# Moving most of the attention output projection into the last attention unit

## The chip, the cores and the metric

The kernel runs on one core of a Trainium2 chip. The metric is the device time of one execution in microseconds (us), median of several runs. Profiled times come from one execution that the hardware profiler recorded.

## The reference

The input is x of shape (4, 1024, 128): 4096 rows of 128 features. The model is

```
x = x + 0.5 * FFN(layernorm(x))
x = x + Attention(layernorm(x))
x = x + 0.5 * FFN(layernorm(x))
```

Both feed-forward steps use the same weights. FFN has a gate (8 experts, the two best of each row by a sigmoid score), eight experts of width 64, `silu(x Wg) * (x Wu)` and a down product, masked by the choice and scaled by one mean weight per expert, plus a shared expert of width 128. Attention has 16 query heads and 4 key heads of size 8, a causal mask and a bias that is linear in the distance with a slope per head. Its 128 output features go through `out @ Wo + bo`. All values are float32. Layernorm has no weights, only mean, variance and `1/sqrt(v + 1e-5)`.

## The kernel before

**Tiling.** The 4096 rows are 32 tiles of 128, in 8 groups of 4 tiles (512 rows, `GROUPS`, `GT`). The 4 batches and 4 key heads give 16 attention units (`UNITS`); unit i belongs to batch i // 4. Batch b holds groups 2b and 2b + 1. Each engine has its own written-out instruction stream, and semaphores order them. An engine executes its stream strictly in order, so an instruction that waits holds back all behind it. PSUM has 8 banks of 128x512 float32.

**Stages.** First feed-forward up (`ffn_up(f1, ...)`) and down (`ffn_down(f1, True)`), the latter with the projections to queries, keys and values; attention (`attention`); output projection (`out_proj`); second feed-forward (`ffn_up(f2, ...)`, `ffn_down(f2, False)`).

**An attention unit** has 12 steps (`STEPS`): four key tiles for the first 512 queries and eight for the second 512. In step s TensorE (PE) computes, at lines 1270 to 1304, the scores of step s + 1 in two pairs of heads (`score`, banks 3 to 6); between them maxima work of the next unit (`piece`, ring of banks 0 to 2), which the last unit, 15, hasn't; then the products of the exponentials of step s - 2 with the values (`times_v`, bank 7, `LAG` = 2). ScalarE (ACT) computes one exponential per pair (line 653) and copies bank 7 out when half a unit is complete (`out_evac`, line 642: for the unit before in step 3, for the first half of this one in step 6). A pair of scores may only be written when the exponential of the same pair of the step before has read the bank. `out_T` (steps 4 and 6, line 1220) turns the copied outputs, and VectorE (DVE) divides them by the row sums into `attn` (`normalise`, line 977). In unit 15 VectorE has little else to do. After the last unit come `times_v` of its last two steps, its last `out_evac`, `out_T` and `normalise`.

**Output projection** (`out_proj`, DVE lines 1019 to 1045, PE lines 1310 to 1326, ACT lines 663 to 668). For each group c: `gather` (DVE) brings 512 rows of `attn` into `sg`, `attention_T` (PE, four 128x128 transposes) turns them, ACT copies them to `yT`, PE multiplies by `wo` (four products of 128 columns), and `residual` (DVE) adds them to x. All of it waits for the last `normalise` (`dve.wait_ge(a_on, 2 * UNITS)`). Groups alternate between two banks each for turned outputs and for products.

**Second feed-forward, up.** In `front` group c has `statistics` (DVE, `ln_stats`, line 718), `rsqrt` (POOL), `ln_apply` (DVE, line 730), four transposes (PE), a copy to `xnT_all` (ACT, line 585), the gate's `logits` (PE) and up to two tiles of products `up(k)` (PE: one for `wg` and one for `wu`, 512 columns each, `front_tiles(c)`: none for group 0, one for group 1, two for each later group), `silu` (ACT) and `hidden` (DVE, line 746). The remaining tiles follow the eight groups. Tiles come in the order `TILE_ORDER`, whose first tiles belong to group 0. `xn` has room for one group, so `ln_apply` of a group waits for the transposes of the one before. `keep_running(n)` (PE, line 1328) issues n products of 512 columns whose result nobody reads: five ahead of the second feed-forward, two behind its first transposes.

Of the kernel before, what the change touches and what calls it, by code (L numbers as in the profile page):

```python
# [12 lines left out]
P = 128  # L13
# [71 lines left out]
WARM_FIRST, WARM_SECOND = 3, 5  # L85
# [35 lines left out]
W0_STEP = 5  # L121

# [54 lines left out]
def macaron(nc, dram, out):  # L177
    ctx = ExitStack()
    with ctx:
# [153 lines left out]
        def bank(b):  # L333
            return ps[:, b, :]

# [220 lines left out]
        def _(act):  # L556
# [20 lines left out]
            def ffn_up(f, load_constants):  # L577
                def silu(k, b):
                    act.wait_ge(f.G, k + 1)
                    after(act, f.h, k - 1)  # L580
                    act.activation(sg[:, b, :], bank(3 + b), ACT.Silu).then_inc(f.sg, 1)  # L581

                def front(c, par, first, last):
                    act.wait_ge(f.T, c + 1)
                    act.activation(xnT_all[:, c, :], bank(7 * par), copy).then_inc(f.xA, 1)
                    for k in front_tiles(c):
                        silu(k, k % 2)
                    if load_constants and c == GROUPS - 2:
                        constants()

                over_groups(front)
                act.wait_ge(f.lg, GROUPS)
                act.activation(sc, lg, ACT.Sigmoid).then_inc(f.sig, 1)
                for k in range(FRONT_END, len(TILE_ORDER)):
                    if k == SEL_AT:
                        act.wait_ge(f.mT, 1)
                        act.activation(selT.rearrange("p a n -> p (a n)"), ps[:, 2, 0:P].bitcast(BF16), copy)\
                           .then_inc(f.mk, 1)
                    silu(k, k % 2)
# [63 lines left out]
            def out_proj():  # L663
                def body(c, par, first, last):
                    act.wait_ge(o_T, c + 1)
                    after(act, o_y, c - 1)
                    act.activation(yT[:, par, :], bank(par), copy).then_inc(o_aT, 1)
                over_groups(body)

            ffn_up(f1, True)  # L670
# [3 lines left out]
            out_proj()  # L674
            ffn_up(f2, False)
# [4 lines left out]
        def _(dve):  # L680
# [57 lines left out]
            def ffn_up(f, first_ffn):  # L738
                ch = Chain(dve, f.ch_up)
                LN_LINKS, TOP_LINKS = 2, 17  # L740
# [8 lines left out]
                def statistics(c, par):  # L749
                    ch.at(LN_LINKS * c)  # L750
                    if first_ffn:
                        dve.wait_ge(s_x[c], 16)
                    ln_stats(c, par, ch, f.ve)
# [91 lines left out]
                statistics(0, 0)  # L845
# [13 lines left out]
            def ffn_down(f, qkv):  # L859
                ch = Chain(dve, f.ch_down)  # L860
                LN_LINKS, SPLIT_LINKS = 2, 2
# [114 lines left out]
            def attention(last_split):  # L976
# [42 lines left out]
            def out_proj():  # L1019
                def gather(c, b, half, par):  # L1020

                    after(dve, o_T, c - 1)
                    src = attn[:, bass.ds(KVH * b, KVH), GT * half:GT * half + GT, :]
                    dve.tensor_copy(sg[:, par, :].rearrange("p (t g e) -> p g t e", t=GT, g=KVH), src)\
                       .then_inc(o_an, 1)

                def residual(c, par):
                    dve.wait_ge(o_y, c + 1)
                    dve.tensor_tensor(xt(c), xt(c), bank(2 + par).rearrange("p (t f) -> p t f", t=GT), V.add)\
                       .then_inc(o_x, 1)  # L1030

                dve.wait_ge(a_on, 2 * UNITS)
                dve.wait_ge(o_bo, BO_PARTS)
                gather(0, 0, 0, 0)
                gather(1, 0, 1, 1)
                gather(2, 1, 0, 0)
                residual(0, 0)
                gather(3, 1, 1, 1)
                residual(1, 1)
                for b in range(1, BATCH - 1):  # L1040
                    gather(2 * b + 2, b + 1, 0, 0)
                    residual(2 * b, 0)
                    gather(2 * b + 3, b + 1, 1, 1)
                    residual(2 * b + 1, 1)
                residual(GROUPS - 2, 0)
                residual(GROUPS - 1, 1)
                dve.wait_ge(o_x, GROUPS)

            ffn_up(f1, True)
            last_split = ffn_down(f1, True)  # L1050
            attention(last_split)
            out_proj()
            ffn_up(f2, False)
# [4 lines left out]
        def _(pe):  # L1058
# [9 lines left out]
            def ffn_up(f, between):  # L1068
                def up(k):
                    b = k % 2  # L1070
                    c, tile = TILE_ORDER[k]
                    xT = xnT_all[:, c, :]
                    after(pe, f.sg, k - 1)
                    mm(bank(3 + b), wg[:, tile, :], xT).then_inc(f.G, 1)
                    after(pe, f.h, k - 1)
                    mm(bank(5 + b), wu[:, tile, :], xT).then_inc(f.U, 1)

                def logits(c, par):
                    pe.wait_ge(f.xA, c + 1)
                    after(pe, f.lg, c - 1)  # L1080
                    for t in range(GT):
                        ins = mm(ps[:, 1 + par, EXPERTS * t:EXPERTS * t + EXPERTS], xnT_all[:, c, t * P:(t + 1) * P],
                                 gate_w[:, :])
                    ins.then_inc(f.gl, 1)

                def front(c, par, first, last):
                    pe.wait_ge(f.xn, c + 1)
                    after(pe, f.xA, c - 1)
                    turn(lambda t: xn[:, t, :], 7 * par).then_inc(f.T, 1)
                    if first:  # L1090
                        keep_running(between)
                    else:
                        logits(c - 1, 1 - par)
                    if c == 1:
                        pe.wait_ge(s_w, 16 * len(ffn_loads))
                    for k in front_tiles(c):
                        up(k)
# [16 lines left out]
                logits(GROUPS - 1, 1)  # L1114
                for k in range(FRONT_END, len(TILE_ORDER)):
# [4 lines left out]
                    up(k)  # L1120
# [137 lines left out]
            def attention():  # L1258
# [11 lines left out]
                def body(i, par, first, last):  # L1270
# [8 lines left out]
                    for s in range(NSTEP):  # L1279
# [20 lines left out]
                        if s == OT0_STEP:  # L1300
                            out_T(i, 0)
                        if s == W0_STEP and not last:
                            maxima_T(i + 1, 0)

                over_units(body)
# [4 lines left out]
            def out_proj():  # L1310
                def attention_T(c, par):
                    pe.wait_ge(o_an, c + 1)
                    after(pe, o_aT, c - 1)
                    turn(lambda t: sg[:, par, t * P:(t + 1) * P], par).then_inc(o_T, 1)

                def body(c, par, first, last):
                    if not last:
                        attention_T(c + 1, 1 - par)
                    pe.wait_ge(o_aT, c + 1)
                    after(pe, o_x, c - 1)  # L1320
                    for t in range(GT):
                        ins = mm(ps[:, 2 + par, t * P:(t + 1) * P], yT[:, par, t * P:(t + 1) * P], wo[:, :])
                    ins.then_inc(o_y, 1)

                attention_T(0, 0)
                over_groups(body)
# [9 lines left out]
            ffn_up(f1, 3)  # L1336
# [3 lines left out]
            out_proj()  # L1340
            keep_running(WARM_SECOND)
# [59 lines left out]
```

## Time and profile before

| | us |
|---|---|
| median of 3 runs | 728.12 (727.83 to 728.29) |
| profiled execution, its own time | 728.65 |
| its span, from first to last instruction | 726.8 |
| TensorE busy | 699.3 (96%) |
| VectorE busy | 567.9 (78%) |
| ScalarE busy | 406.6 (56%) |
| GpSimd busy | 139.6 (19%) |

Busy time is what an engine spent in instructions, a TensorE matmul counted up to a modelled end. The shares are averages over stages with different limits. The attention stage ends shortly before 589 us, the output projection at 601, the second feed-forward with the end.

### The profile page before, as it was taken

Reading aid. Unit: us, or ns where it says so; the run is one execution under the profiler, and the core shown is the slowest. Engines: PE = TensorE matmul, PEld = TensorE weight load, DVE = VectorE, ACT = ScalarE, POOL = GpSimd, SP = SyncE. Lnnn points to the kernel's source line nnn. Section 1 sums busy time; section 2 is a strip of 40 time slices with the busy share of each in tenths; the row PEclk is TensorE's granted clock in tenths of the full one; section 3 lists DMA queues with packets and bytes.
Section 4 is the critical chain, followed back from the end, with each engine's and each line's share of the span. In section 5 each row is a group of like instructions: output and inputs, shape, how many; then the busy total and the mean of one; then the engine's idle time right before and its main releaser. Section 6 shows DMA issues by size and latency. Waiting matters only on the chain.

```text
span 726.8 us, 15935 instructions
## 1 busy us (share of the span) xinstructions
PE 699.3 (96%) x5906; PEld 364.1 (50%) x5906; DVE 567.9 (78%) x1880; ACT 406.6 (56%) x587; POOL 139.6 (19%) x157
## 2 busy tenths in 40 slices
PE   8999999979999999999999999999999789999998
PEld 4554498833344444444444444444444265544597
DVE  6976338697999999999999999999999148775311
ACT  3353353224776777777777677777767843353200
POOL 3202895552000000000000000000000002104950
PEclk9999999965999999999999999999999999999999
DMA  8014533443001001100100110010010000005651
GB/s 221 1 17 75 92 70 115 142 150 105 21 21 39 21 22 38 39 21 21 39 21 21 39 31 25 24 39 21 21 40 1 2 1 1 1 1 100 107 87 59
DMA packets 47249, 34.69 MB, mean 48 GB/s; under 512 B 13106, under 2 KB 46514, under 8 KB 47172
## 3 DMA queue, kind: packets, MB, share of 16 engines
q1 hardware_dynamic: 46596, 33.60, 19.3%
q8 instruction: 47, 0.77, 0.5%
q14 instruction: 30, 0.25, 0.1%
q10 hardware_dynamic: 576, 0.08, 0.1%
HBM read 23.01 MB, written 10.39 MB: 46 GB/s over the span
## 4 chain that ended last, share of the span: by engine, by line
PE 59%; DVE 16%; issue 13%; DMA 4%; SPq 3%; POOL 3%; ACT 2%; DVEq 0%; ACTq 0%; POOLq 0%
PE ps L1060 55%; DVE mx L945 8%; PE ps L1065 4%; POOL h_all L495 2%; DMA mask_second<-sel_scr 2%; DVE mx L938 1%; ACT h_all L653 1%; DMA yT<-sel_scr 1%; DVE xn L734 1%; DMA k_scr<-kp 1%; SPq L392 1%; DVE stats L722 1%; DVE h_all L938 1%; SPq L389 1%; DVE wb L965 1%
## 5 line engine op out<-in xcount | busy, mean ns | idle before, releaser
L653 ACT ACTIVATE h_all<-ps 128x1024 f32<-128x1024 f32 (+3 forms) x384 | 291.3, 810 | 108.3 <-PE ps L1060 105.2
L945 DVE TENSOR_REDUCE mx<-ps 128x1 f32<-128x512 f32 (+2 forms) x352 | 223.0, 681 | 9.5 <-PE ps L1060 6.5
L1060 PE MATMUL ps<-ks,xnT_all 57*128 57x512 bf16 (+3 forms) x768 | 178.0, 337 | 10.5 <-DVE mx L938 4.7
L1060 PE MATMUL ps<-h_all,vb 128*32 128x512 f32 (+3 forms) x1536 | 163.9, 500 | 0.6 <-ACT osb L642 0.6
L1060 PE MATMUL ps<-xnT_all,ks 59*128 59x512 bf16 (+3 forms) x768 | 158.6, 332 | 3.3 <-ACT h_all L653 3.2
L938 DVE CUSTOM_DVE_ANT_0 h_all<-ps,mask_w 128x384 bf16<-128x384 f32 (+1 forms) x256 | 149.2, 618 | 4.1 <-issue 2.4
L1060 PEld LDWEIGHTS ps<-ks,xnT_all 57*128 57x128 bf16 x768 | 56.3, 94 | 137.7 <-DVE mx L938 63.3
L1060 PE MATMUL ps<-cb 64*128 64x64 bf16 (+3 forms) x1216 | 112.5, 215 | 0.0
L746 DVE TENSOR_TENSOR h_all<-ps,sg 128x512 f32<-128x512 f32 x80 | 55.2, 690 | 50.0 <-PE ps L1060 48.3
L581 ACT ACTIVATE sg<-ps 128x512 f32<-128x512 f32 x80 | 47.8, 597 | 82.6 <-PE ps L1060 82.3
L1060 PEld LDWEIGHTS ps<-cb 64*128 64x128 bf16 x1216 | 80.1, 96 | 17.0 <-issue 0.4
L1060 PE MATMUL ps<-xnT_all,wg 128*128 128x512 f32 x160 | 83.3, 602 | 0.0
L1060 PE MATMUL ps<-xnT_all,wu 128*128 128x512 f32 x160 | 81.7, 592 | 0.0
L1060 PE MATMUL ps<-wds,h_all 128*128 128x128 f32 x640 | 74.9, 276 | 0.0
L1060 PEld LDWEIGHTS ps<-wds,h_all 128*128 128x128 f32 x640 | 72.8, 192 | 2.8 <-issue 2.6
L538 POOL COPY vb<-v_all 128x64 f32<-128x64 f32 x16 | 3.7, 238 | 356.1 <-PE ps L1060 356.1
L1060 PEld LDWEIGHTS ps<-xnT_all,ks 59*128 59x128 bf16 x768 | 45.0, 93 | 42.6 <-ACT h_all L653 26.2
L1060 PEld LDWEIGHTS ps<-h_all,vb 128*32 128x32 f32 x1536 | 30.6, 108 | 38.1 <-issue 29.1
L1060 PEld LDWEIGHTS ps<-xnT_all,wu 128*128 128x128 f32 x160 | 30.4, 190 | 38.3 <-issue 38.0
L482 POOL TENSOR_TENSOR rstd<-ve,mhalf 128x4 f32<-128x4 f32 x24 | 24.2, 1010 | 113.6 <-DVE ve L728 113.5
L1060 PEld LDWEIGHTS ps<-xnT_all,wg 128*128 128x128 f32 x160 | 28.9, 190 | 28.7 <-issue 28.7
L495 POOL TENSOR_TENSOR h_all<-h_all,attn 128x512 f32<-128x512 f32 x24 | 27.1, 1166 | 67.7 <-DVE h_all L746 35.5
(128 smaller groups left out, 552.8 us busy)
## 6 DMA issues: line engine op xcount, KB each, us to landing
xnT_all<-q_scr SPq DMA_DIRECT2D x64, 96.0 KB
attn<-sel_scr SPq DMA_DIRECT2D x12, 256.0 KB, 6.8
mask_second<-sel_scr SPq DMA_DIRECT2D x12, 256.0 KB, 7.7
q_scr<-qp SPq DMA_DIRECT2D x8, 384.0 KB
ks<-k_scr SPq DMA_DIRECT2D x64, 48.0 KB
x<-in_x SPq DMA_DIRECT2D x8, 256.0 KB, 5.9
yT<-sel_scr SPq DMA_DIRECT2D x8, 256.0 KB, 9.0
q_scr<-qp SPq DMA_DIRECT2D x8, 256.0 KB
```

The source lines that it names most:

```text
L389: sp.dma_start(q_scr[b, :, r:r + products, n], qp[:, par, part, None, :].broadcast_to([P, products, GN])).then_inc(dw, 16)
L392: sp.dma_start(k_scr[b, :, r + m, n].rearrange("k (t n) -> t k n", t=GT), kp[:, par, m])\
L482: pool.tensor_tensor(rstd[:, par, :], ve[:, par, :], mhalf[:, :], ALU.pow).then_inc(rs_sem, 1)
L495: pool.tensor_tensor(h_all[:, c, tiles, :], h_all[:, c, tiles, :], expert_mask[b][:, tiles, :], ALU.mult).then_inc(f.hm, 1)
L581: act.activation(sg[:, b, :], bank(3 + b), ACT.Silu).then_inc(f.sg, 1)
L653: act.activation(pr[:, (NSTEP * i + s) % PR_BUFS, p:HPG:SLOTS, lo:HALF], ps[:, b:b + 2, lo:HALF], ACT.Exp)\
L722: ins = dve.bn_stats(stats[:, par, t, :], x[:, c * GT + t, :])
L746: dve.tensor_tensor(h_all[:, TILE_ORDER[k][0], TILE_ORDER[k][1], :], bank(5 + b), sg[:, b, :], V.mult)\
L938: dve.tensor_tensor_reduce(out=junk, in0=ps[:, b, 0:w], in1=mask_w[:, HALF - w:HALF], scale=1.0, scalar=LOWEST, op0=V.add, op1=V.max, accu ...
L945: dve.tensor_reduce(m, src, AX.X, V.max).then_inc(a_out, 1)
L1060: return pe.matmul(o, l, r, start=start, stop=stop, skip_group_check=True)
L1065: ins = pe.transpose(ps[:, b, t * P:(t + 1) * P], src(t), ident)
```

## The change

The output projection of groups 0 to 5 (`EARLY_OUT` = 6) is issued inside the steps of unit 15. With step s as the step of the unit, TensorE gets `attention_T(s - 1)` in steps 1 to 6 and `out_product(s - 2)` in steps 2 to 7, behind the step's scores and `times_v`; VectorE gets the gathers, the copy of the turned outputs to `yT` (`turned_outputs`, which ScalarE did before) and the residual. Turned outputs of groups 0 to 5 use bank 2; products use bank 1 (groups 0 to 3) and bank 0 (groups 4 and 5). In steps 8 to 11 VectorE computes the statistics of groups 0, 1, 2 and applies those of groups 0 and 1, and TensorE turns the rows of group 0 in step 10. Behind the last `times_v` come `logits` of group 0, the last `out_T`, the rows of group 1, the first tile `up(0)`, and then the transposes and products of groups 6 and 7. ScalarE copies the turned rows of group 0 ahead of its last `out_evac`, those of group 1 behind it. `ffn_up` of the second feed-forward begins with group 2 on TensorE. The `keep_running` calls of the second feed-forward are gone; those of the first stay at three.

```diff
-WARM_FIRST, WARM_SECOND = 3, 5
+WARM_FIRST, WARM_BETWEEN = 3, 3
+EARLY_OUT = 6
+STATS_STEP = 8
+ROWS_READY = 3
...
+        def out_banks(c):
+            if c < EARLY_OUT:
+                return 2, 1 if c < EARLY_OUT - 2 else 0
+            return ((0, 6), (4, 7))[c - EARLY_OUT]
...
                 over_units(body)
+                turned_rows(f2, 0, 0)
                 out_evac(UNITS - 1, 1)
+                turned_rows(f2, 1, 1)
+            def last_outputs():
+                for c in range(EARLY_OUT, GROUPS):
+                    act.wait_ge(o_T, c + 1)
+                    after(act, o_y, c - 1)
+                    act.activation(yT[:, c % 2, :], bank(out_banks(c)[0]), copy).then_inc(o_aT, 1)
...
                 def front(c, par, first, last):
-                    if not last:
+                    if not last and c + 1 >= rows_ready:
                         statistics(c + 1, 1 - par)
-                    ln_apply(c, par, f.rs, f.T, f.xn)
+                    if c >= rows_ready:
+                        ln_apply(c, par, f.rs, f.T, f.xn)
...
+            def turned_outputs(c):
+                dve.wait_ge(o_T, c + 1)
+                after(dve, o_y, c - 1)
+                dve.tensor_copy(yT[:, c % 2, :], bank(out_banks(c)[0])).then_inc(o_aT, 1)
...
+                def beside_last_unit(s):
+                    if s == 0:
+                        dve.wait_ge(o_bo, BO_PARTS)
+                        gather(0)
+                        gather(1)
+                    if 2 <= s < EARLY_OUT + 2:
+                        residual(s - 2)
+                    if 1 <= s < EARLY_OUT + 1:
+                        turned_outputs(s - 1)
+                    if 1 <= s < EARLY_OUT - 1:
+                        gather(s + 1)
+                    if s == STATS_STEP:
+                        second_statistics(ch, 0, 0)
+                    if s == STATS_STEP + 1:
+                        second_statistics(ch, 1, 1)
+                        ln_apply(0, 0, f2.rs, f2.T, f2.xn)
+                    if s == STATS_STEP + 2:
+                        second_statistics(ch, 2, 0)
+                    if s == STATS_STEP + 3:
+                        ln_apply(1, 1, f2.rs, f2.T, f2.xn)
...
                 over_units(body)
                 normalise(UNITS - 1, 1)
                 dve.wait_ge(a_on, 2 * UNITS)
+                for c in range(EARLY_OUT, GROUPS):
+                    gather(c)
+                ln_apply(2, 0, f2.rs, f2.T, f2.xn)
+                for c in range(EARLY_OUT, GROUPS):
+                    residual(c)
...
                 def front(c, par, first, last):
+                    if c < done:
+                        return
+                    if done and c == 3:
+                        pe.wait_ge(o_x, GROUPS)
...
+                    if done and c == 2:
+                        pe.wait_ge(o_x, EARLY_OUT + 1)
...
                         if s == OT0_STEP:
+                            if last:
+                                pe.wait_ge(o_x, EARLY_OUT - 2)
                             out_T(i, 0)
...
+                        if last:
+                            beside_last_unit(s)
                 over_units(body)
                 for s in range(NSTEP - LAG, NSTEP):
                     times_v(UNITS - 1, s, 1)
+                pe.wait_ge(a_on, 2 * UNITS - 1)
+                logits(f2, 0, 0)
                 out_T(UNITS - 1, 1)
+                rows_T(f2, 1, 1)
+                for k in front_tiles(1):
+                    up(f2, k)
+                for c in range(EARLY_OUT, GROUPS):
+                    attention_T(c)
+                for c in range(EARLY_OUT, GROUPS):
+                    out_product(c)
+            def beside_last_unit(s):
+                if s == EARLY_OUT:
+                    pe.wait_ge(a_on, 2 * UNITS - 2)
+                if 2 <= s < EARLY_OUT + 2:
+                    out_product(s - 2)
+                if s == 1:
+                    pe.wait_ge(a_wc, 2 * UNITS)
+                if 1 <= s < EARLY_OUT + 1:
+                    attention_T(s - 1)
+                if s == STATS_STEP + 2:
+                    pe.wait_ge(o_x, EARLY_OUT)
+                    rows_T(f2, 0, 0)
...
-            out_proj()
-            keep_running(WARM_SECOND)
             ffn_up(f2, 2)
```

## Rows read from the trace of the kernel before

**Rows 1.** The chain that ended last, 560 to 727: start us, us, what
```profile
586.88 0.61 ACT osb L642
...
587.62 0.64 PE ps L1065 x4
...
608.09 0.66 PE ps L1065 x4
```

**Rows 2.** Busy time of the engines in stretches, then granted clock, DMA share, GB/s
```profile
567.36:586.85 19.49, 16.01 (x184) 5.63 (x180) 1.10 (x4) 14.69 (x21) 0.00 (x0) 1.00 0.01 1
586.85:600.92 14.07, 11.84 (x101) 11.40 (x102) 8.24 (x17) 5.28 (x9) 0.00 (x0) 1.00 0.00 1
...
611.19:723.33 112.14, 112.13 (x561) 74.29 (x559) 52.87 (x150) 30.34 (x50) 39.86 (x36) 1.00 0.31 55
```

**Rows 3.** Waits of TensorE, 562 to 587: total us, times, longest us
```profile
PE ps L1060 <- ACT h_all L653: 3.2, 7, 1.0
PE ps L1060 <- ACT osb L642: 0.6, 1, 0.6
```

**Rows 4.** Groups of instructions, 586.85 to 601: busy us, mean ns, idle before
```profile
L1029 DVE TENSOR_TENSOR x<-x,ps 128x512 f32<-128x512 f32 x8 | 5.5, 688 | 3.9 <-PE ps L1060 3.9
L1065 PE MATMUL ps<-c,sg 128*128 128x128 f32 x32 | 4.7, 275 | 1.2 <-DVE sg L1024 1.2
L667 ACT ACTIVATE yT<-ps 128x512 f32<-128x512 f32 x8 | 4.7, 598 | 7.5 <-PE ps L1065 7.5
...
L1024 DVE COPY sg<-attn 128x512 f32<-128x512 f32 x8 | 3.3, 422 | 0.5 <-PE ps L1065 0.4
```

**Rows 5.** Timeline of unit 15, TensorE: start us, us, line, operation
```profile
567.36 0.23 PE L1060 MATMUL ps<-xnT_all,ks 59*128 59x128 bf16 x2
...
569.79 0.61 PE L1060 MATMUL ps<-xnT_all,ks 59*128 59x512 bf16 x4
570.33 0.85 PE L1060 MATMUL ps<-h_all,vb 128*32 128x384 f32 x8
...
573.76 0.74 PE L1060 MATMUL ps<-xnT_all,ks 59*128 59x512 bf16 x4
...
577.05 1.07 PE L1060 MATMUL ps<-h_all,vb 128*32 128x512 f32 x8
578.05 0.66 PE L1065 MATMUL ps<-c,osb 128*128 128x128 f32 x4
578.64 0.39 PE L1060 MATMUL ps<-xnT_all,ks 59*128 59x512 bf16 x2
579.35 1.07 PE L1060 MATMUL ps<-h_all,vb 128*32 128x512 f32 x8
...
584.45 2.36 PE L1060 MATMUL ps<-h_all,vb 128*32 128x512 f32 x32
```

**Rows 6.** Timeline of the output projection, TensorE
```profile
592.23 1.06 PE L1060 MATMUL ps<-wo,yT 128*128 128x128 f32 x8
...
593.12 0.61 PE L1065 MATMUL ps<-c,sg 128*128 128x128 f32 x4
...
593.57 1.06 PE L1060 MATMUL ps<-wo,yT 128*128 128x128 f32 x8
```

**Rows 7.** Timeline of the second feed-forward, transposes of groups 2 and 3
```profile
611.19 0.60 PE L1065 MATMUL ps<-c,xn 128*128 128x128 f32 x4
...
615.96 0.60 PE L1065 MATMUL ps<-c,xn 128*128 128x128 f32 x4
```

**Rows 8.** Timeline, VectorE: statistics and application
```profile
603.08 0.29 DVE L722 BATCH_NORM_STATS2 stats<-x 128x6 f32<-128x128 f32 x1
...
604.48 1.11 DVE L734 TENSOR_SCALAR xn<-x,mv,rstd 128x128 f32<-128x128 f32 x4
```

**Rows 9.** Stretches around the only fall of the clock, columns as rows 2
```profile
150.00:151.00 1.00, 0.20 (x1) 0.09 (x1) 0.97 (x3) 0.44 (x1) 0.92 (x3) 1.00 0.55 162
...
152.00:185.00 33.00, 28.81 (x142) 12.54 (x142) 27.54 (x91) 10.97 (x18) 9.97 (x14) 0.50 0.37 111
```

More of the change, by code:

```diff
@@ L575, in stack_constants, with turned_rows, ffn_up @@
                 act.wait_ge(s_cb, 3)
-            def ffn_up(f, load_constants):
+            def turned_rows(f, c, par):
+                act.wait_ge(f.T, c + 1)
+                act.activation(xnT_all[:, c, :], bank(7 * par), copy).then_inc(f.xA, 1)
+            def ffn_up(f, load_constants, turned):
                 def silu(k, b):
@@ L583, in front @@
                 def front(c, par, first, last):
-                    act.wait_ge(f.T, c + 1)
-                    act.activation(xnT_all[:, c, :], bank(7 * par), copy).then_inc(f.xA, 1)
+                    if c >= turned:
+                        turned_rows(f, c, par)
                     for k in front_tiles(c):
@@ L844, in ffn_up @@
                 slopes = []
-                statistics(0, 0)
+                if not rows_ready:
+                    statistics(0, 0)
                 over_groups(front)
@@ L974, in early_maxima, with gather, residual, attention @@
                         maxima(0, 0)
-            def attention(last_split):
+            def gather(c):
+                after(dve, o_T, c - 1)
+                b, half = c // 2, c % 2
+                src = attn[:, KVH * b:KVH * b + KVH, GT * half:GT * half + GT, :]
+                dve.tensor_copy(sg[:, half, :].rearrange("p (t g e) -> p g t e", t=GT, g=KVH), src)\
+                   .then_inc(o_an, 1)
+            def turned_outputs(c):
+                dve.wait_ge(o_T, c + 1)
+                after(dve, o_y, c - 1)
+                dve.tensor_copy(yT[:, c % 2, :], bank(out_banks(c)[0])).then_inc(o_aT, 1)
+            def residual(c):
+                dve.wait_ge(o_y, c + 1)
+                dve.tensor_tensor(xt(c), xt(c), bank(out_banks(c)[1]).rearrange("p (t f) -> p t f", t=GT), V.add)\
+                   .then_inc(o_x, 1)
+            def attention(last_split, ch):
+                def beside_last_unit(s):
[18 more added lines that the diff above has]
+                        ln_apply(1, 1, f2.rs, f2.T, f2.xn)
                 def normalise(i, j):
@@ L1017, in attention @@
                 normalise(UNITS - 1, 1)
[L1019 to L1030, printed above, removed]
-                dve.wait_ge(a_on, 2 * UNITS)
[L1033 to L1049, printed above, removed]
+                dve.wait_ge(a_on, 2 * UNITS)
+                for c in range(EARLY_OUT, GROUPS):
[3 more added lines that the diff above has]
+                    residual(c)
+            ffn_up(f1, True, Chain(dve, f1.ch_up), 0)
             last_split = ffn_down(f1, True)
-            attention(last_split)
-            out_proj()
-            ffn_up(f2, False)
+            second = Chain(dve, f2.ch_up)
+            attention(last_split, second)
+            ffn_up(f2, False, second, ROWS_READY)
             ffn_down(f2, False)
@@ L1066, in turn, with up @@
                 return ins
[L1068 to L1084, printed above, removed]
-                def front(c, par, first, last):
-                    pe.wait_ge(f.xn, c + 1)
-                    after(pe, f.xA, c - 1)
-                    turn(lambda t: xn[:, t, :], 7 * par).then_inc(f.T, 1)
+            def up(f, k):
+                b = k % 2
+                c, tile = TILE_ORDER[k]
+                xT = xnT_all[:, c, :]
+                after(pe, f.sg, k - 1)
+                mm(bank(3 + b), wg[:, tile, :], xT).then_inc(f.G, 1)
+                after(pe, f.h, k - 1)
+                mm(bank(5 + b), wu[:, tile, :], xT).then_inc(f.U, 1)
@@ new lines, in logits, with rows_T @@
+            def logits(f, c, par):
+                pe.wait_ge(f.xA, c + 1)
+                after(pe, f.lg, c - 1)
+                for t in range(GT):
+                    ins = mm(ps[:, 1 + par, EXPERTS * t:EXPERTS * t + EXPERTS], xnT_all[:, c, t * P:(t + 1) * P],
+                             gate_w[:, :])
+                ins.then_inc(f.gl, 1)
+            def rows_T(f, c, par):
+                pe.wait_ge(f.xn, c + 1)
+                after(pe, f.xA, c - 1)
+                turn(lambda t: xn[:, t, :], 7 * par).then_inc(f.T, 1)
@@ L1303, in body @@
                             maxima_T(i + 1, 0)
+                        if last:
+                            beside_last_unit(s)
                 over_units(body)
@@ L1307, in attention, with attention_T, out_product @@
                     times_v(UNITS - 1, s, 1)
+                pe.wait_ge(a_on, 2 * UNITS - 1)
+                logits(f2, 0, 0)
                 out_T(UNITS - 1, 1)
[L1310 to L1326, printed above, removed]
+                rows_T(f2, 1, 1)
[5 more added lines that the diff above has]
+                    out_product(c)
+            def attention_T(c):
+                pe.wait_ge(o_an, c + 1)
+                after(pe, o_aT, min(c, EARLY_OUT))
+                turn(lambda t: sg[:, c % 2, t * P:(t + 1) * P], out_banks(c)[0]).then_inc(o_T, 1)
+            def out_product(c):
+                pe.wait_ge(o_aT, c + 1)
+                after(pe, o_x, min(c, EARLY_OUT))
+                for t in range(GT):
+                    ins = mm(ps[:, out_banks(c)[1], t * P:(t + 1) * P], yT[:, c % 2, t * P:(t + 1) * P], wo[:, :])
+                ins.then_inc(o_y, 1)
+            def beside_last_unit(s):
+                if s == 0:
+                    assert len(ring.emptied) % RING == 0
+                if s == EARLY_OUT:
[9 more added lines that the diff above has]
+                    rows_T(f2, 0, 0)
             def keep_running(n):
```

42 lines of the change are left out of this document (23 added, 19 removed).

## The prediction

> **What bounds the kernel now.** I read the chain that ended last first, to find which engine carries the stretch around the edit [rows 1]. It runs from the last evacuation of attention (586.88) over the transpose at 587.62 and a hand-over ladder to 608.09, where the second transposes of the second feed-forward start; the reader is to see that between the end of attention and that row no engine works at its capacity. The windows come second [rows 2]: in unit 15 TensorE is busy 16.01 of 19.49 us, VectorE 1.10 us. In the out-projection TensorE shows 11.84 of 14.07 us. From 611.19 to 723.33 it shows 112.13 of 112.14 us: there it is the bound, so every microsecond by which this stretch starts earlier is a microsecond of the end. The waits come third [rows 3]: in unit 15 TensorE waits 3.8 us (3.2 + 0.6) for ScalarE. That is all the slack into which more TensorE work can fall; VectorE's slack there is 18 us.
>
> So I measure the change at one instruction: the transposes of rows of group 3 in the second feed-forward, at 615.96 [rows 7]. What comes behind has the same instructions in the same order. The sum is made in the profiled execution: span 726.8 us, its own time 728.65 us (1.85 us lie around the span), 0.53 us above the median of 728.12; I take the saving off the median.
>
> **Prices.** One group of out-projection costs TensorE 1.34 us when nothing is waited for (592.23 to 593.57) [rows 6]: 0.89 us of products, to 593.12, and 0.45 of transposes. Reading the same rows, a matmul's record overruns what follows by about 0.17 us, so the last products of attention (584.45 + 2.36, 32 matmuls of four steps) leave TensorE free at 586.64 [rows 5]. VectorE's residual is 0.69 us, ScalarE's copy of turned outputs 0.60 [rows 4]. The same copy on VectorE is not in the trace: between 0.42 (its gather of the same size, out of SBUF, same rows) and 0.69 (the residual, which reads PSUM too); I take 0.65, since it reads PSUM. Statistics of a group take VectorE 1.40 us (603.08 to 604.48), its application 1.11 [rows 8]. In unit 15 the pieces are [rows 5]: both score pairs 0.54 (569.79 to 570.33), 0.71 with a full diagonal (578.64 to 579.35); products with V 1.00 (577.05 to 578.05), by width 0.78, 0.57, 0.36 for narrower ones (estimates, 0.21 less for each 128 columns); a transpose group ahead of scores 0.59 (578.05 to 578.64).
>
> **Unit 15, step by step.** Added: six groups at 1.33 plus one group of row transposes at 0.44, 8.4 us of TensorE. I place the first scores of each step; of the old starts, rows 5 show steps 2, 3, 5 and 7.
> Step 1 gets only a transpose group: step 2 starts at 567.90 (was 567.36). The evacuation it waits for moves too, V's products of step 2 start at 569.4, and from there each of steps 2 to 6 carries a whole group (1.33, and 0.1 for the turn to bf16). Step 3: 571.85 (was 569.79, +2.1). Step 4: 574.6. Step 5: 577.6 (573.76, +3.85), its length 0.54 + 0.36 + 1.43, plus 0.1 in which the product waits for VectorE (residual 0.69 and copy 0.65 behind product 2, against 1.44 us of TensorE's own work between). Step 6: 580.0; its second score pair waits for an exponential, and part of the delay is absorbed. Step 7: 583.9 (578.64, +5.3). Step 8: 586.6, behind product 5. Step 9: about 588.3, where an exponential is waited for again. V's products of step 10 end at 591.25 (was 585.3).
> There TensorE wants the rows of group 0. VectorE: residual 5 ends at 587.4, two statistics and one application (1.40, 1.40, 1.11) give 591.3. That is a wait of about 0.1 us; the transposes end at 591.85, and the last three products at 593.2, against 586.64. Growth of unit 15: **6.6 us** for 8.4 us of work.
> Bounds: all 3.8 us of waits used, growth 4.6; none used, and 0.1 us of wait at each of ten hand-overs, growth 9.4. ScalarE's moved copies cost nothing here (it has no copy of groups 0 to 5 left; VectorE's slack hides them), its row copy of group 0 fits between its last exponential and the evacuation. POOL's power of 1.0 us per group lies beside the second statistics. SP's queue gets and loses nothing.
>
> **Behind attention.** From the free TensorE at 0: logits of group 0 (0.89) lie under the evacuation that the old kernel also waited for (586.88 + 0.61, next transpose 587.62 [rows 1], 0.98 after the free point). Then transposes 0.44, rows of group 1 0.44 (ready), first tile 1.72: 3.58. Normalisation (0.6, an estimate from two small instructions) and gather 6 (0.42) lie under the tile. Transposes 6 and 7; the product of 6 starts 1.35 after transposes 6 began (0.61 of the record, 0.60 of the copy, hand-overs): 4.93. Two products, 1.78: **6.71**. Then rows of group 2.
> The old kernel had its rows of group 2 at 611.19, 24.55 us behind its free point. The out-projection's ladder, the serial residual, statistics and application, and the warming matmuls go. So the gain at group 2 is 24.55 - 6.71 - 6.6 = 11.2 us.
>
> **What is late next.** From group 2 to group 3 TensorE needs 4.77 us (611.19 to 615.96). VectorE now does more in it: residual 7 ends 0.9 after the product, then statistics 3 (1.40), logits 0.2 and hidden 0 0.69 (estimates; the second moves as much as a residual), statistics 4 (1.40), application 3 (1.11) and a hand-over: 5.8 us. In the old kernel residual and statistics 3 were already done. So **1.0 us** of wait, once: afterwards VectorE has about 4.2 us of work per 4.77 us. Bounds: 0 (if I count a statistics too dear and the copy is short) and 2.0 (one more operation late). Should the first tile be late, its cover of normalisation and gather goes, 1.0 us, within these bounds.
> Saving: 11.2 - 1.0 = 10.2 us; 728.12 - 10.2 = **717.9 us**.
>
> **Rivals.**
> A, unit 15 hides nothing. The growth is 9.4 instead of 6.6, so 728.12 - 7.4 = 720.7. For it: the waits of rows 3 are for exponentials whose scores themselves move later when TensorE is delayed, so that ScalarE idles and the slack reappears elsewhere. Against: ScalarE is busy 14.7 of the 19.5 us [rows 2], so TensorE can run ahead of it.
> B, the slack is used up and VectorE is on time: growth 4.6, no wait at group 3: 728.12 - 13.2 = 714.9. Against: 0.6 of the 3.8 us is for an evacuation that stays [rows 3], and VectorE would have to be 1.0 us faster than its rows.
> C, the other side: the ladder inside unit 15 becomes serial. There is one bank for turned outputs and one for products (groups 0 to 3), so transposes, copy, product and residual of a group could follow each other: 0.66 + 0.65 + 1.06 + 0.69 and hand-overs, 3.2 us. Six of them and the rows are 19.6 us of growth: 24.55 - 6.71 - 19.6 - 1.0 = -2.8, so 730.9 us. It decides from 2.7 us on the path per group. Against: the product of c stands a step behind its transposes, with scores and V's products between (at least 0.9 us), so only step 5's is close.
> D, the clock falls to 1.2 GHz, as it did around 151 us, where TensorE had been busy 0.20 of a microsecond, and then granted 0.50 for 33 us with 28.81 us busy [rows 9]; half of that is 14.4 us, giving 717.9 + 14.4 = 732.3. For it: the five warming matmuls behind the out-projection and two more go. Against: the out-projection, transposes and products of 128 columns alone, kept 1.00 over 14.07 us [rows 2], 32 of them transposes [rows 4], and the longest waits I find are about 1 us.
> The Trainium skill, page "TensorE: Matmul & The Clock Gate", Part 4, says that transposes do not count as activity for the clock. By that rule the seven transpose groups now put into unit 15 are as good as idle time; no row here shows a fall from it, since scores and V's products stand between them.
> E, the change does not do what it says (a wait of the last unit keeps the out-projection behind attention): 728. Against: groups 0 to 5 read units 0 to 11 only, all normalised long before.
>
> **How the numbers follow.** My forecast 717.9 (716.0 to 719.5 by itself) 0.60; A 0.20; B 0.12; C 0.03; D 0.02; E 0.03. The range runs from B's 714.9 to 9.4 growth with 2.0 us of wait, 728.12 - 6.4 = 721.7. A measurement of this kernel can tell 0.2% (1.5 us) from no change. Faster by more: 0.60 + 0.20 + 0.12 and a little of C with only part of the groups serial, 0.93; within 0.2%: 0.03; slower: 0.04.
>
> **What would show it.** In the new trace: first scores of step 7 about 5 us later than now; the last V products 6 to 7 us later; a wait of TensorE for VectorE's rows of group 3 near 1 us and none at group 4; first tile under the normalisation; the clock at 1.00 throughout; from group 3 on the same times, shifted by 10. Wrong if TensorE waits for copies of turned outputs in most steps (C), if steps 2 to 6 grow by over 1.5 us each (A), or if the group 3 wait recurs.

## The result and the profile after

The changed kernel takes 715.96 us (median of 4 runs, 714.09 to 717.27) beside 727.98 for the kernel before on the same chip: ratio 0.9847, 95% interval 0.9824 to 0.9870. Five more runs on another occasion gave 716.61 (715.17 to 720.05) beside 726.76: 0.9856, 0.9833 to 0.9879. Over all its 9 runs the median is 716.61, over 33 runs of the kernel before 726.75: 10.1 us, or 1.4%. Forecast was 717.9, a gain of 10.2.

Executions of the kernel before differ among each other by up to 7 us (724.36 to 731.26). The profiled spans of the two kernels differ by 14.5 (712.3 against 726.8), more than the medians do. So the traces are compared from a fixed point on: the copy of the last maxima for unit 15 on VectorE, the last event of the steady stage. First the kernel before, then the changed one (timeline: start us, us, engine, line, operation).

```profile
566.37 0.21 DVE L954 COPY wt<-ps 32x128 bf16<-32x128 bf16 x1 [0.94 <-PE ps L1217]
```
```profile
562.03 0.21 DVE L978 COPY wt<-ps 32x128 bf16<-32x128 bf16 x1 [0.93 <-PE ps L1269]
```

4.34 us of the 14.5 lie ahead of this point, where both kernels do the same; 10.15 behind. Now the changed kernel's rows that answer to [rows 5, 7]: the first scores of step 7, the last products with V, the second feed-forward's transposes of groups 2 and 3.

```profile
579.62 0.39 PE L1103 MATMUL ps<-xnT_all,ks 59*128 59x512 bf16 x2
...
587.78 1.50 PE L1103 MATMUL ps<-h_all,vb 128*32 128x384 f32 x24
...
595.93 0.60 PE L1108 MATMUL ps<-c,xn 128*128 128x128 f32 x4
...
601.47 0.63 PE L1108 MATMUL ps<-c,xn 128*128 128x128 f32 x4 [0.61 <-issue]
```

| us behind the copy of the maxima | before | changed | predicted step | measured |
|---|---|---|---|---|
| TensorE free of the last V product | 20.27 | 27.08 | growth 6.6 | 6.81 |
| transposes of group 2 | 44.82 | 33.90 | 6.71 behind that | 6.82 |
| transposes of group 3 | 49.59 | 39.44 | 5.8, with 1.0 of wait | 5.54, with 0.77 |
| gain | | | 10.2 | 10.15 |

(Free means the end of the record less 0.17, as in the prediction.) Unit 15, the part behind it, and the part from group 2 to group 3 as stretches of the changed kernel: busy times in the order PE, PEld, DVE, ACT, POOL, then granted clock.

```profile
562.03:589.11 27.08, 25.81 (x276) 14.35 (x272) 16.80 (x63) 16.53 (x24) 2.54 (x3) 1.00 0.01 2
589.11:595.93 6.82, 6.57 (x52) 5.22 (x45) 3.40 (x11) 3.70 (x6) 0.49 (x1) 1.00 0.00 0
595.93:601.47 5.54, 4.93 (x22) 2.70 (x21) 5.18 (x31) 2.25 (x4) 2.00 (x2) 1.00 0.00 0
```

TensorE now carries the first two: 25.81 of 27.08 and 6.57 of 6.82. VectorE went from 1.10 of 19.49 us in [rows 2] to 16.80 of 27.08 and still has slack there. In the third stretch (TensorE 4.93 of 5.54) VectorE, with 5.18, is the one waited for. The waits of TensorE say the same; this view answers to [rows 3], but begins at the fixed point.

```profile
PE ps L1103 <- ACT osb L655: 1.0, 1, 1.0
PE ps L1108 <- issue: 0.6, 1, 0.6
PE ps L1103 <- ACT yT L682: 0.2, 1, 0.2
```

The waits for exponentials have left this list (3.2 us in [rows 3], of which 2.8 lie behind the fixed point). Two short ones remain in the timeline, which the list doesn't show: the scores of step 6 take 0.83 us where those of step 5 take 0.61, and those of step 9 take 0.79 (584.02 to 584.81) where the kernel before took 0.50 (582.56 to 583.06). The wait for the evacuation grew from 0.6 to 1.0. The row "issue 0.6" is the wait at group 3. The view names no releaser; VectorE's application ran from 600.25 to 601.37, just ahead of 601.47, and e2 tests that it is the cause.

### The profile page after: what moved, and what is told of

Same layout as the page of the kernel before. It is cut to its first block, busy times and chain, and to the rows that moved or that the text cites. A ratio compares the mean times of both kernels' runs of the same rounds, so it can differ in the third digit from the quotient of the medians.

```text
span 712.3 us, 15912 instructions
## 1 busy us (share of the span) xinstructions
PE 688.1 (97%) x5892; PEld 359.0 (50%) x5892; DVE 569.5 (80%) x1886; ACT 403.1 (57%) x581; POOL 139.1 (20%) x157
## 4 chain that ended last, share of the span: by engine, by line
PE 60%; DVE 15%; issue 13%; DMA 4%; SPq 3%; POOL 2%; ACT 2%; DVEq 0%; ACTq 0%; POOLq 0%
PE ps L1103 56%; DVE mx L969 8%; PE ps L1108 4%; POOL h_all L504 2%; DMA mask_second<-sel_scr 2%; DVE mx L962 1%; DMA yT<-sel_scr 1%; DMA k_scr<-kp 1%; SPq L401 1%; DVE xn L748 1%; DVE h_all L962 1%; ACT h_all L666 1%; SPq L398 1%; DVE stats L736 1%; DVE wb L989 0%
## 5 line engine op out<-in xcount | busy, mean ns | idle before, releaser
L1103 PE MATMUL ps<-ks,xnT_all 57*128 57x512 bf16 (+3 forms) x768 | 176.3, 333 | 10.1 <-DVE mx L962 5.1
```

The lines of the kernel that those rows point to most:

```text
L1103: return pe.matmul(o, l, r, start=start, stop=stop, skip_group_check=True)
```

## Experiments

The measure of each is the stretch from the copy of the maxima to the transposes of group 3, from one profile, beside the timed ratio to the kernel before, run on the same occasion (medians 727.98 for the first comparison, 726.76 for e1 to e4, 726.90 for e5 to e8, 726.49 for e9 and e10).

| run | stretch, us | median, us | ratio to before, interval |
|---|---|---|---|
| before, 33 runs | 49.59 | 726.75 | |
| changed | 39.44 | 715.96 | 0.9847 (0.9824 to 0.9870) |
| e1 again | 39.44 | 716.61 | 0.9856 (0.9833 to 0.9879) |
| e2 statistics of 3 earlier | 38.67 | 715.89 | 0.9835 (0.9815 to 0.9856) |
| e3 out-projection only | 47.56 | 724.07 | 0.9956 (0.9939 to 0.9974) |
| e4 before, no warming | 55.89 | 732.65 | 1.0066 (1.0046 to 1.0086) |
| e5 both waits filled | 37.79 | 715.89 | 0.9847 (0.9831 to 0.9864) |
| e6 products doubled | 44.57 | 721.21 | 0.9930 (0.9903 to 0.9956) |
| e7 all behind unit 15 | 56.67 | 735.07 | 1.0112 (1.0093 to 1.0130) |
| e8 copies on ScalarE | 39.72 | 715.38 | 0.9848 (0.9819 to 0.9877) |
| e9 both, busy stage | 37.79 | 716.33 | 0.9860 (0.9828 to 0.9892) |
| e10 both again | 37.79 | 715.70 | 0.9843 (0.9808 to 0.9878) |

**e1, the changed kernel again.** No edit.

> The changed kernel unaltered. Its first profile had unit 15 begin 3.98 us earlier than the kernel before (first scores at 558.73 against 562.71), and only 10.5 us of the 14.5 us of shorter span behind that point. Theory 1 (chance): the 3.98 us are how long TensorE's clock stayed at half rate between 150 and 190 us in this one execution (mean granted clock 0.988 against 0.977) and are no effect of the change; then in another profile the start of unit 15 moves by some us with the mean clock, the stretch from there to the rows of group 3 stays 42.7 us (within 0.1), and the time over five rounds is 10.5 to 11 us below the kernel before at equal mean clock. Theory 2 (effect): something in the changed program makes the earlier stages shorter; then unit 15 begins at 559 again and the median gain is 14.

The stretch is 39.44 again, and the copy of the maxima came at 564.17 instead of 562.03. In the other runs it came between 563.12 and 566.90, the latest with a variant of the changed kernel. So the 4.34 us is no effect of the change. The gain, 10.15 us at the medians, is a little under the 10.5 to 11 that theory 1 gave. The scatter goes loosely with the clock of the stage from 150 to 190 us, whose mean was 0.79 in the first profile of the changed kernel, 0.70 here and 0.57 in that of the kernel before; but four profiles with the same 0.62 (e2, e4, e5, e8) have the copy of the maxima anywhere from 563.87 to 566.90. In the first profile of the changed kernel:

```profile
150.00:160.00 10.00, 5.21 (x32) 2.70 (x32) 9.87 (x28) 1.82 (x4) 6.47 (x10) 0.85 0.45 134
160.00:170.00 10.00, 8.04 (x35) 3.38 (x33) 7.11 (x23) 3.70 (x6) 3.62 (x7) 0.67 0.49 144
170.00:180.00 10.00, 9.81 (x74) 4.03 (x77) 9.34 (x38) 5.17 (x8) 1.45 (x3) 0.63 0.34 101
```

against 0.50 in [rows 9].

**e2, statistics of group 3 ahead of the residuals.**

```diff
                 ln_apply(2, 0, f2.rs, f2.T, f2.xn)
+                second_statistics(ch, 3, 1)
...
-                    if not last and c + 1 >= rows_ready:
+                    if not last and c + 1 >= rows_ready + (not first_ffn):
```

> Statistics of group 3 are issued on VectorE behind the application of group 2, ahead of the residuals of groups 6 and 7, where the changed kernel's VectorE waits 1.96 us for the product of group 6. Theory 1 (TensorE waits at the rows of group 3 because VectorE has 1.40 us of these statistics behind the residuals): the stretch from the rows of group 2 to those of group 3 falls from 5.54 to 4.77 us, 0.7 us in all. Rival (the wait is set by POOL's power or by the chain of the tile's silu and hidden): it stays at or above 5.3.

Group 2 to group 3 takes 4.77 us (598.45 to 603.22); the wait is gone. The cause named for it, too much on VectorE between the two, holds. The median is 0.7 us lower than in e1, less than the scatter of either.

**e3, only the out-projection is moved.** The rows, logits and tile of the second feed-forward leave unit 15 and its tail, and the warming returns.

```diff
-                    if s == STATS_STEP:
-                        second_statistics(ch, 0, 0)
...
-                pe.wait_ge(a_on, 2 * UNITS - 1)
-                logits(f2, 0, 0)
...
-                rows_T(f2, 1, 1)
-                for k in front_tiles(1):
-                    up(f2, k)
...
+            pe.wait_ge(o_x, EARLY_OUT + 1)
+            keep_running(5)
+            ffn_up(f2, 0)
```

> Keeps the out-projection of groups 0 to 5 inside unit 15 and that of groups 6 and 7 behind, but begins the second feed-forward after it, as the kernel before does, with its warming matmuls (five and two). Theory 1 (most of the gain is the serial residual, statistics and application behind the out-projection): unit 15 grows by 6.0 us, groups 6 and 7 with their residual take 6.9 us behind the last product with V, then 6.5 to the second transposes, 3.1 and 4.77 to the rows of group 3, 21.2 us in all against 12.36 in the changed kernel: 8.4 us slower than the changed kernel and only about 2.4 us faster than the kernel before. Rival (the moved out-projection itself is the gain): at least 7 us faster than before.

The stretch is 47.56: the moved out-projection alone is worth 2.0 us (expected about 2.4), and what e3 takes back is worth 8.1 on top of it (expected 8.4). Those 8.1 us are of three edits at once, the early rows of groups 0 to 2, the first tile ahead of groups 6 and 7, and the warming left out; no run separates them, and the early rows need the moved out-projection. The chain that was on the path stays there, between the residual of group 7 and the transposes of group 1 (timeline of e3):

```profile
595.73 0.69 DVE L1015 TENSOR_TENSOR x<-x,ps 128x512 f32<-128x512 f32 x1 [0.21 <-PE ps L1091]
...
599.14 1.11 DVE L746 TENSOR_SCALAR xn<-x,mv,rstd 128x128 f32<-128x128 f32 x4
...
602.84 0.63 PE L1096 MATMUL ps<-c,xn 128*128 128x128 f32 x4 [0.16 <-DVE xn L746]
```

These are 7.1 us in which TensorE has only group 0's transposes and the warming.

**e4, the kernel before without its second warming.**

```diff
-            keep_running(WARM_SECOND)
-            ffn_up(f2, 2)
+            ffn_up(f2, 0)
```

> The kernel before without the five and two warming matmuls of the second feed-forward. Theory 1: TensorE then idles about 4.5 us for VectorE, whose chain sets the start of the front anyway; if the granted clock stays at 1.00 the time is the same within 0.3 us. Rival D of the prediction (the clock falls): a granted clock of 0.50 behind 605 us for up to 33 us and up to 14.4 us more. If it falls here, the changed kernel is saved from it by having no such gap, and its removal of the warming is free only together with the rest.

5.9 us slower at the median, 6.3 in the stretch. The stretches show the granted clock (third column from the end):

```profile
575.00:578.00 3.00, 3.00 (x20) 1.16 (x14) 0.52 (x2) 1.00 (x2) 0.00 (x0) 0.50 0.02 5
...
589.00:591.00 2.00, 2.00 (x11) 1.76 (x10) 0.43 (x1) 1.19 (x2) 0.00 (x0) 0.50 0.00 0
...
600.00:605.00 5.00, 1.07 (x10) 0.88 (x8) 4.39 (x26) 0.00 (x0) 1.15 (x2) 1.00 0.00 2
605.00:610.00 5.00, 2.87 (x13) 2.48 (x13) 4.85 (x31) 1.19 (x2) 2.15 (x3) 0.55 0.00 0
610.00:615.00 5.00, 5.00 (x13) 2.83 (x13) 1.30 (x5) 1.88 (x2) 0.74 (x1) 0.50 0.00 0
615.00:620.00 5.00, 5.00 (x21) 3.04 (x20) 3.41 (x19) 1.79 (x3) 1.01 (x1) 0.92 0.01 2
```

Without the warming TensorE was busy 1.07 of 5 us, with a single wait of 4.73 us, and then its clock was 1.2 GHz for about 10 us. So rival D's mechanism is real. But the first two lines show that in this execution the clock also fell twice ahead of the edit, in unit 15 and at the start of the out-projection, where the instructions are those of the kernel before. The transposes of group 0, the first instruction behind the gap, come 41.93 us behind the copy of the maxima against 39.27 before: 2.7 of the 6.3 us are lost by then. From there to group 3 it is 13.96 against 10.32, so the gap costs 3.6 us in this trace. Why the median is 5.9 us higher isn't shown; its six runs have mean clocks of 0.967 to 0.972, below every run of the kernel before on that occasion (0.976 to 0.986).

In the profiles of the changed kernel, e1, e2, e5, e6 and e8 to e10 the clock is 1.00 from the copy of the maxima to group 3, with no warming there: without the gap it can be left out.

**e5, the wait for the evacuation filled too.** On top of e2:

```diff
+            def ahead_of_values(s):
+                if s == 1:
+                    pe.wait_ge(a_wc, 2 * UNITS)
+                    attention_T(0)
+                if s == 2:
+                    out_product(0)
+                    attention_T(1)
...
+                        if last:
+                            ahead_of_values(s)
                         if s >= LAG:
                             times_v(i, s - LAG, par)
```

> The changed kernel with two edits: the statistics of group 3 ahead of the residuals of 6 and 7 (as before, 0.77 us), and in unit 15 the transposes of group 0 ahead of the products with V in step 1, the product of group 0 and the transposes of group 1 ahead of them in step 2, where TensorE waits 0.97 us for the evacuation of bank 7. Theory 1 (TensorE is the bound of unit 15, so a filled wait is worth its length): from the copy of the maxima (the last before unit 15's steps) to the rows of group 3 37.8 us, 39.44 - 0.77 - 0.9, and about 1.6 us less time than the changed kernel. Rival (the wait reappears, since group 0's copy on VectorE, 0.69 us, ends later than the evacuation): 38.6.

37.79, as expected (37.8). Of the three waits that the changed kernel's list shows only 0.2 remains, and 0.4 came up for an exponential. The median is 0.7 us below that of e1 and not 1.6, within the scatter.

**e6, the six products doubled.**

```diff
-                for t in range(GT):
+                for t in (*range(GT), *range(GT if c < EARLY_OUT else 0)):
                     ins = mm(ps[:, out_banks(c)[1], t * P:(t + 1) * P], yT[:, c % 2, t * P:(t + 1) * P], wo[:, :])
```

> In the changed kernel each of the six out-projection products inside unit 15 is computed twice into the same bank (8 more matmul instructions, 0.89 us each group, 5.3 us in all), with nothing else changed. Theory 1 (after the change unit 15 is bound by TensorE; the slack of 3.8 us it had is used up): the stretch from the copy of the maxima to the rows of group 3 grows by 5.0 to 5.4 us, from 39.44 to 44.6. Rival (slack is left in unit 15, ScalarE's exponentials still set its length): grows by 3 us or less.

5.13 us for 5.3 us of added work (the median is 4.6 above that of e1). Unit 15 is bound by TensorE after the change: the rival with slack left is excluded.

**e7, the same work behind unit 15.** The calls beside the steps are issued behind the last product with V.

```diff
                 over_units(body)
                 for s in range(NSTEP - LAG, NSTEP):
                     times_v(UNITS - 1, s, 1)
+                pe.wait_ge(a_on, 2 * UNITS - 1)
+                for s in range(NSTEP):
+                    beside_last_unit(s)
```

> The work that the changed kernel issues beside the steps of unit 15 is issued behind its last product with V, in the same order and on the same engines; the wait for bank 1 is the normalisation of unit 15's first half. Theory 1: unit 15 is as short as before the change (6.8 us less), but TensorE's 8.4 us come behind it at VectorE's pace (residual 0.69, copy 0.69, gather 0.42: 1.8 us a group, 10.8 for six), and the two statistics and the application ahead of group 0's transposes (3.9 us) and the ones ahead of group 1's stand open: 39.4 - 6.8 + 10.8 + 0.9 + 3.9 + 2.5 = 50.7 us from the copy of the maxima to the rows of group 3, about as long as the kernel before (49.59), and more if the clock falls in the 4 us gap. Rival (the new order alone, groups 6 and 7 behind the first tile, is what gains; the place beside unit 15 is worth only the 1.6 us of waits used): 41 to 43 us.

56.67, against 50.7 expected and 41 to 43 by the rival: with the same instructions 17.2 us behind the changed kernel, the place beside unit 15 is what makes the change a gain, and my own number was 6 short. Two causes are visible. First, a group takes 2.54 us, not 1.8:

```profile
589.67 1.16 PE L1103 MATMUL ps<-wo,yT 128*128 128x128 f32 x8 [0.94 <-DVE yT L1012]
...
590.87 0.69 DVE L1017 TENSOR_TENSOR x<-x,ps 128x512 f32<-128x512 f32 x1 [0.92 <-PE ps L1103]
591.47 0.69 DVE L1012 COPY yT<-ps 128x512 f32<-128x512 f32 x1
...
592.21 1.16 PE L1103 MATMUL ps<-wo,yT 128*128 128x128 f32 x8 [0.94 <-DVE yT L1012]
```

Product, residual and, behind it in VectorE's order, the next copy form a ring: 589.67 to 592.21. The bank of the products is not what closes it: from product 3 to product 4, which change banks, it takes 2.59 us (594.75 to 597.34), and the waits name the copy (L1012). This is rival C's ladder without cover, 0.74 us a group over my 1.8, 4.4 us. Second, the gap that followed let the clock fall:

```profile
600.00:605.00 5.00, 1.00 (x8) 0.81 (x8) 3.80 (x26) 0.00 (x0) 1.32 (x2) 0.69 0.00 2
605.00:610.00 5.00, 3.51 (x16) 3.17 (x17) 2.93 (x18) 1.08 (x2) 1.71 (x2) 0.50 0.00 0
```

Of the remaining 1.6 us, 1.4 lie between the transposes of group 0 and of group 2 (605.71 to 616.46, 10.75 us against 9.32 by my sum), over which the clock is at half rate until about 612; from group 2 on it is 5.53 as in the changed kernel. So some 1.4 of the 17.2 us are the clock's.

**e8, copies by ScalarE.**

```diff
-                    if 1 <= s < EARLY_OUT + 1:
-                        turned_outputs(s - 1)
...
+                            if last and p == 1 and 2 <= s < EARLY_OUT + 2:
+                                turned(s - 2)
```

> The copies of turned outputs of groups 0 to 5 are made by ScalarE (0.60 us), behind the second exponential of the step, and not by VectorE (0.69). Theory 1 (in unit 15 both engines have slack beside TensorE, and only the product of step 5 waits about 0.1 us for VectorE's copy): the same within 0.3 us. Rival (a copy ahead of the next exponential delays it, so that TensorE waits for ScalarE again): 1 to 3 us longer.

0.28 us longer in the stretch, no difference in time. The rival's mechanism shows in small: TensorE waits for exponentials again, twice, 0.7 us in all. Which engine copies has hardly any weight.

**e9, TensorE kept busy in the earlier stage.** On top of e5, eleven unread products.

```diff
+            def stay_busy(n):
+                for _ in range(n):
+                    mm(bank(7), ones[:, :], wd[:, 0:MT, :].rearrange("p a n -> p (a n)"))
```

> The kernel with both waits filled, and eleven products of 512 columns whose result nobody reads (bank 7) where TensorE waits for VectorE at the end of the first feed-forward's down stage (one ahead of the transposes of group 6, one ahead of each of the five pieces of maxima work there, two ahead of the first maxima transposes, one in the next pieces, two in the pieces ahead of attention). In nine profiles so far the copy of the maxima of unit 15 came anywhere from 562.0 to 566.9, whatever the kernel, with the granted clock at 0.50 in some 20 to 33 us of the stretch 150 to 190. Theory 1 (that scatter and some of the stage is the clock's fall behind TensorE's waits of 0.7 to 1.7 us): the clock stays at 1.00, the copy of the maxima comes at 556 to 560 and the time falls by 4 to 9 us to some 707 to 711, with less scatter. Rival (VectorE is the bound there, TensorE's half rate is hidden, or the added products delay it as much as they give): no change or up to 5 us slower.

The clock held until 170 (1.00 and 1.00 from 150 to 170, 0.66 from 170 to 180; mean 0.990 to 0.995 over the five runs, against 0.975 to 0.978 in e10). The copy of the maxima came at 565.34, in e10 at 565.32: no gain, against 4 to 9 us expected. The rival is right that this stretch does not pay for TensorE's clock when it costs such products; which part is VectorE's bound and which the products' own time stays open. It also narrows the reading of e1: over the 33 runs of the kernel before the time falls as the mean clock rises (correlation -0.80), but holding the clock with added products did not lower the time, so the clock as the cause of the scatter is not shown.

**e10, both waits filled, again.** The kernel of e5, no further edit.

> The kernel with both waits filled, again, for the time that one profile could not settle: from the copy of the maxima to the rows of group 3 it is 1.65 us shorter than the changed kernel (37.79 against 39.44). Theory 1: the same 37.8 us there, and a median of 714 to 716. Rival (the scatter of the earlier stage covers 1.65 us): a median within 1 us of the changed kernel's 716.6.

715.70 us, stretch 37.79. The median fits theory 1 (714 to 716) and the rival (within 1 us of 716.6) alike. The nine runs of e5 and e10 have a median of 715.76 beside 716.61 for the nine of the changed kernel. 1.65 us less is shown by the traces; the times agree in direction, but cannot tell it from no change. The version has the shortest stretch found, by the trace.

## Why the prediction was right

**Where the gain sits.** The prediction measured at the transposes of group 3 and took all behind as unchanged. From 601.47 on the groups follow in 4.77 to 4.79 us, as before, and the end of the span comes 110.83 us behind (before: 110.84). The 10.15 us add up so: the kernel before spent 24.55 us from its last product with V to the rows of group 2, and the changed one needs 8.4 us (an estimate from the prices) in unit 15 and 6.82 behind it for the same work. That leaves 9.3 us, in which TensorE waited or ran unread products. Unit 15 hid another 1.6 of its 8.4, and the wait at group 3 took 0.8 back. So most of the gain is waits that went away, and little of it is work that became free.

**Growth of unit 15.** 6.6 us was predicted, 6.81 measured; the first scores of step 7 come 17.59 us behind the copy of the maxima against 12.27 [rows 5], 5.3 later as predicted. The remaining waits for exponentials in steps 6 and 9 are those that the prediction placed there. The bound by TensorE's own work is shown by e6. VectorE's copy costs 0.69 us, not 0.65 (row "L1012", mean 685 ns), its upper bound. The wait for it in step 5 came out as 0.1 us. One reading was off: the 3.8 us of [rows 3] called the slack of unit 15 begin at 562, and behind the fixed point they are 3.4, so the lower bound of the growth was 5.0 and not 4.6.

**Rival A** (all 8.4 and more on the path) is out: the growth lies 1.6 us under the work. Its mechanism, waits that reappear elsewhere, remains in small in the two short waits of steps 6 and 9 and in the evacuation's 1.0.

**Rival B** is half right: the wait at group 3 can go (e2), but it needs an edit.

**Rival C** did not occur, and was priced too high: a fully serial group costs 2.54 us (e7), not 3.2, because the transposes of the next group run beside the residual and are no step of the ring. By its own point of decision (2.7 us) the ladder alone would not have made the kernel slower.

**Rival D.** Right in mechanism for a kernel with the gap (e4, e7), with 3.6 us behind it and not 14.4: the clock returned after some 10 us and not 33. It did not come: in the changed kernel the granted clock is 1.00 in all three stretches. But one argument against it was weaker than it looked: the out-projection kept 1.00 in the one profile of the kernel before, and in e4 the same instructions were at 0.50 from 589 to 591. The Trainium skill, page "TensorE: Matmul & The Clock Gate", Part 4, says that transposes do not count as busy time for the clock in the way that other matmuls do. Seven groups of them in unit 15 of the changed kernel, among other products, went with a clock of 1.00, so the rule was not tested here.

**The size.** Each term was right to about 0.2 us; that the sum is right to 0.1 is luck, as the errors cancel. The growth was 0.21 too low. The part behind it was 0.11 too low, all of it in the two products of groups 6 and 7 (594.04 to 595.93, 1.89 us and not 1.78). The wait at group 3 was 0.23 too high, most of it in the logits and hidden on VectorE (598.14 to 598.85, 0.71 us and not 0.89). The time itself is 1.9 us under the forecast 717.9, or 1.3 over all nine runs: the saving was taken off 728.12, the median of three runs, and 33 runs give 726.75. The gain of 12.0 in the first comparison is 10.1 over all runs; the difference is of the size of the scatter ahead of the fixed point.

## What to carry to other kernels

When a section is a chain of hand-overs, ask how much of it is waiting and not work, and issue it beside a stage in which the engines that it waits for have room. Here only 1.6 of 8.4 us of moved TensorE work was hidden; the rest of the gain is waits that went. Follow the chain past the section that you move: moving the out-projection alone gave 2.0 us, and bringing the first rows of the next stage forward with it 8.1 more. Warming products are a price for a gap; close the gap and they go, but don't take them out of a kernel that still has it (3.6 us lost behind the gap in e4's trace, 5.9 at the median). Compare traces from a fixed event next to the edit when an earlier stage scatters by more than the edit's terms.

## What the runs showed of the hardware

In e4 TensorE had 1.07 us of work between 600 and 605, and a wait of 4.73 us, before its granted clock fell from 1.00 to 0.50 near 605.5. It was back at 1.00 near 616, some 10 us later; TensorE was busy 2.87 us from 605 to 610 and throughout from 610 to 615. In e7 it fell near 602, one us into a wait of 4.71 us, and was back near 612. Shorter waits give no such clear picture. With single waits of 1.0 us or less in unit 15 of the changed kernel the clock stayed at 1.00, and so it did in e7 from 585 to 600, where TensorE was busy 9.45 of 15 us with waits of 0.8 to 1.0 us. But in unit 15 of the unchanged kernel, with waits of 0.47 and 1.01 us just ahead, it stayed at 1.00 in the profile of the kernel before and fell for some 3 us in e4. The same instructions with the same waits can meet either clock, so one profile at 1.00 doesn't show that a stretch is safe. Holding the clock up in the earlier stage from 150 to 170 with added products gave nothing (e9, 565.34 against 565.32); how much a low clock costs there by itself is not shown.
